# One core, a two-layer attention and feed-forward stack: the last layer's back pieces split in halves, one feed-forward unit per pair of heads, TensorE's back products one pair later, and two copies on ScalarE in the other order

## The reference, cut to what matters

```python
x = in_features                                   # (8, 512, 128) float32
x = x + attn_a(layernorm(x))                      # 1: attention over the full width, causal
x = x + ffn(layernorm(x))                         # 2
x = x + attn_b(layernorm(x), Wq, Wk, Wv, Wo, gamma, beta)   # 3: 16 heads of 64, causal
x = x + ffn(layernorm(x))                         # 4

def attn_b(x, ...):      # per head h: q, k, v = x Wq[h], x Wk[h], x Wv[h]
    attn = softmax(causal(q k^T / 8)); heads = concat(attn v)
    y = x + heads @ Wo
    return (y - mean(y)) * rsqrt(var(y) + 1e-3) * gamma + beta

def ffn(x):              # M = 64, INNER = 16
    s = x @ Win + bin_
    h = relu(s[..., None] * W1 + b1)
    return (einsum('btmh,mh->btm', h, W2) + b2) @ Wout + bout
```

## Time and profile before

| what | value |
|---|---|
| median of 3 runs | 915.17 us (912.46 to 921.88) |
| the profiled execution: its time / its span | 914.78 us / 912.9 us |
| granted TensorE clock, mean over the span | 0.905 |
| PE busy | 741.9 us (81%) |
| PEld / DVE / ACT / POOL busy | 533.9 / 659.8 / 571.5 / 533.4 us |
| heads stage: first pair of batch 0 starts / last pair of batch 7 starts | 235.8 / 859.1 us |

### The profile page before, as it was taken

One profiled execution on the slowest core, in us unless ns is written; L12 is line 12 of the kernel. 1 busy time (PEld: TensorE's weight loads), 2 busy tenths in 40 slices (PEclk: granted clock), 3 DMA queues, 4 the chain that ended last, 5 costly groups with the idle time before them and its releaser, 6 DMA issues. The chain is left out here.

```text
span 912.9 us, 21228 instructions
## 1 busy us (share of the span) xinstructions
PE 741.9 (81%) x7592; PEld 533.9 (58%) x7592; DVE 659.8 (72%) x1358; ACT 571.5 (63%) x1575; POOL 533.4 (58%) x496
## 2 busy tenths in 40 slices
PE   4476667633899998999899899989998998998843
PEld 3354555522466765766676567666766765666532
DVE  1488888763666787689678858967896896789654
ACT  0357666651667765776677668667767766776623
POOL 2156666443356567567666756665676667577631
PEclk9598878755999999999999999989999999999965
DMA  9111111101299888798579768959987898798630
GB/s 202 43 43 40 47 47 46 36 26 44 49 150 154 144 144 142 123 137 145 108 133 154 128 112 146 151 104 137 152 137 122 150 141 117 134 152 146 114 72 23
DMA packets 367142, 100.29 MB, mean 110 GB/s; under 512 B 347968, under 2 KB 364864, under 8 KB 367040
## 3 DMA queue, kind: packets, MB, share of 16 engines
q1 hardware_dynamic: 363776, 96.86, 61.6%
q10 hardware_dynamic: 3264, 2.10, 0.9%
HBM read 8.73 MB, written 2.10 MB: 12 GB/s over the span
## 5 line engine op out<-in xcount | busy, mean ns | idle before, releaser
L1003 POOL TENSOR_TENSOR prob_hl<-prob,prob_hl 128x768 f16<-128x768 f32 (+1 forms) x192 | 363.5, 1893 | 231.7 <-DVE prob_hl L947 231.6
L922 ACT ACTIVATE prob<-wide,neg_max 128x128 f32<-128x128 f32 (+3 forms) x512 | 264.8, 527 | 164.3 <-DVE neg_max L959 164.2
L959 DVE TENSOR_REDUCE neg_max<-wide 128x2 f32<-128x256 f32 (+3 forms) x256 | 204.7, 821 | 150.5 <-PE wide L836 149.0
L831 PE MATMUL wide<-k_sb,q_sb 64*128 64x128 f32 (+3 forms) x1024 | 195.2, 480 | 1.6 <-ACT k_sb L813 1.5
L856 PE MATMUL bank<-v_hi,prob_t 128*128 128x64 f16 x1280 | 136.4, 195 | 11.8 <-DMA prob_t<-prob_hl 10.9
L947 DVE CAST prob_hl<-prob 128x768 f16<-128x768 f32 (+1 forms) x192 | 135.9, 708 | 1.8 <-DMA prob_t<-prob_hl 1.0
L857 PE MATMUL bank<-v_lo,prob_t 128*128 128x64 f16 x1280 | 136.2, 195 | 0.0
L858 PE MATMUL bank<-v_hi,prob_t 128*128 128x64 f16 x1280 | 136.1, 195 | 0.0
L856 PEld LDWEIGHTS bank<-v_hi,prob_t 128*128 128x128 f16 x1280 | 118.4, 100 | 15.6 <-issue 11.7
L857 PEld LDWEIGHTS bank<-v_lo,prob_t 128*128 128x128 f16 x1280 | 116.5, 100 | 0.0
L858 PEld LDWEIGHTS bank<-v_hi,prob_t 128*128 128x128 f16 x1280 | 116.5, 100 | 0.0
(11 more groups left out here) (190 smaller groups left out, 1449.4 us busy)
## 6 DMA issues: line engine op xcount, KB each, us to landing
prob_t<-prob_hl SPq DMA_TRANSPOSE x384, 3.1
x_next<-in_L_attn_a_in_features SPq DMA_DIRECT2D x8, 256.0 KB, 3.1
x_attn<-in_L_attn_a_in_features SPq DMA_DIRECT2D x8, 256.0 KB, 3.1
x_sb<-x_done SPq DMA_DIRECT2D x8, 256.0 KB, 2.3
y_res<-bn_y SPq DMA_DIRECT2D x8, 256.0 KB, 2.3
out_x<-x_done SPq DMA_DIRECT2D x8, 256.0 KB, 2.6
wq_a<-in_L_attn_a_w_q ACTq DMA_DIRECT2D x1, 512.0 KB, 5.2
wq_b<-in_L_attn_b_Wq SPq DMA_DIRECT2D x1, 512.0 KB, 8.2
```

The lines of the kernel that those rows point to most:

```text
L831: pe.matmul(dst[:, h, c:c + m], q[e, i * P:(i + 1) * P], k[e, 0:m], start=(i == UNIT_ROWS[u][0]), stop=False)
L922: last = act.activation(prob_2[s][:, at:at + m], score_banks(p, s)[:, h, c:c + m], ACT.Exp, bias=neg_max[p % 2][:, h, i:i + 1], accum_out= ...
L959: last = dve.tensor_reduce(neg_max[p % 2][:, :, i:i + 1], score_banks(p, s)[:, :, c:c + m], AX.X, ALU.max, negate=True)
L1003: pool.tensor_tensor(prob_hl[u][:, w:2 * w], prob_2[u][:, 0:w], prob_hl[u][:, 0:w], ALU.subtract)\
```

## The change

The back's centre and residual on VectorE are cut in two halves of two blocks each, in steps 1 and 2 of p3 and in steps 0 and 1 of p4; the moments leave the statistics and go to step 0 of the next pair. On GpSimd ffn_xb goes behind unit 2 of p4, the second root to p5 unit 0, and the normalised tokens are made in halves behind units 1 and 2 of p5. TensorE's turn goes from p5 to p6, the product with Win from p6 to p7, the product with Wout (with x_done) from p7 to p0 of the next batch; all are still in step 2. The relus and adds of batch b - 2 are one per pair, in step 0: the relu of unit p in pair p, its add in the next pair, at the end of step 0's list on VectorE (the place is before the pieces of the back). Behind the last heads (b = 8) batch 6's units are taken one per step, and its output leaves in p3. On ScalarE the contexts are copied before the keys. DRAIN is one longer. The store follows one pair behind x_done.

```diff
@@ -722,12 +722,23 @@
...
         LAG = 4
-        DRAIN = 2 * HP + 1
-        RELU_PAIRS = (0, 1, 5, 6)
+        DRAIN = 2 * HP + 2
...
+        def unit_of_ffn(b, p, s):
...
+            if b == B:
+                return p * NU + s if p < NU else None
+            return p if s == 0 and 0 <= b - 2 < B else None
...
+        def leaves(b, p):
...
+            if b == B and p == 3:
+                return B - 2
+            return b - 3 if p == 0 and 0 <= b - 3 < B and b - 3 != B - 2 else None
...
@@ -790,11 +801,11 @@
...
             wait(pe, *(("k_sb", n) if done == "q_ps" else ("q_sb", n + 1)))
-            if done == "q_ps" and p == 7:
-                wait(pe, "g_xt", b)
             if done == "q_ps" and p == 0:
+                wait(pe, "g_xt", b - 1)
+            if done == "q_ps" and p == 1:
                 wait(pe, "g_s", b - 1)
-            if done == "q_ps" and p == 1:
+            if done == "q_ps" and p == 2:
...
             split_product(pe, QK, parts[:, p, 0, :], parts[:, p, 1, :], xt_hi[:, at], xt_lo[:, at])\
@@ -894,21 +905,21 @@
...
                         context_turn_tensor(pe, *earlier(b, p, 2))
-                if s == 2 and p == 5 and 0 <= b - 1 < B:
+                if s == 2 and p == 6 and 0 <= b - 1 < B:
                     back_turn_tensor(pe, b - 1)
-                if s == 2 and p == 6 and 0 <= b - 1 < B:
+                if s == 2 and p == 7 and 0 <= b - 1 < B:
                     back_s_tensor(pe, b - 1)
-                if s == 2 and p == 7 and 0 <= b - 2 < B:
-                    back_out_tensor(pe, b - 2)
+                if s == 2 and leaves(b, p) is not None:
+                    back_out_tensor(pe, leaves(b, p))
...
         def heads_scalar(act, b, p):
...
             for s in range(NU):
-                if s == 2 and p == 5 and 0 <= b - 1 < B:
+                if s == 2 and p == 6 and 0 <= b - 1 < B:
                     back_xt_scalar(act, b - 1)
-                if s == 2 and p == 6 and 0 <= b - 1 < B:
+                if s == 2 and p == 7 and 0 <= b - 1 < B:
...
                     wait(act, f"m{s}", n + 1)
@@ -926,16 +937,17 @@
...
                     queries_scalar(act, *later(b, p))
-                if s == 1 and pair_exists(*later(b, p)):
-                    keys_scalar(act, *later(b, p))
...
                     act.copy(ctx_t[:, :], MB[:, :]).then_inc(sem("ctx_t"), 1)
+                if s == 1 and pair_exists(*later(b, p)):
+                    keys_scalar(act, *later(b, p))
...
                     values_scalar(act, b + 1, p, MB)
-                if p in RELU_PAIRS and s < 2 and 0 <= b - 2 < B:
-                    back_relu_scalar(act, b - 2, 2 * RELU_PAIRS.index(p) + s)
+                j = unit_of_ffn(b, p, s)
+                if j is not None and j < J:
+                    back_relu_scalar(act, b - 2, j)
...
@@ -977,22 +989,25 @@
...
                         values_vector(dve, bv + 1, pv, MB)
+                back_adds_vector(dve, b, p, s)
...
                     back_statistics(dve, y_norm, lambda i: y_res[:, (b - 1) * QB + i, :], "gy", b - 1)
-                if s == 1 and p == 3 and 0 <= b - 1 < B:
-                    back_center_vector(dve, b - 1)
-                if s == 0 and p == 4 and 0 <= b - 1 < B:
-                    back_residual_vector(dve, b - 1)
+                if s == 0 and p == 3 and 0 <= b - 1 < B:
+                    back_moments(dve, y_norm, "gy", b - 1)
+                if s > 0 and p == 3 and 0 <= b - 1 < B:
+                    back_center_vector(dve, b - 1, s - 1)
+                if s < 2 and p == 4 and 0 <= b - 1 < B:
+                    back_residual_vector(dve, b - 1, s)
                 if s == 2 and p == 4 and 0 <= b - 1 < B:
-                    wait(dve, "g_x", b)
+                    wait(dve, "g_x", 2 * b)
                     back_statistics(dve, ffn_norm, lambda i: x_ffn[:, i, :], "gf", b - 1)
-                if p in RELU_PAIRS and s > 0 and 0 <= b - 2 < B:
-                    back_add_vector(dve, b - 2, 2 * RELU_PAIRS.index(p) + s - 1)
-                if s == 2 and p == 7 and 0 <= b - 2 < B:
-                    back_done_vector(dve, b - 2)
+                if s == 0 and p == 5 and 0 <= b - 1 < B:
+                    back_moments(dve, ffn_norm, "gf", b - 1)
+                if s == 2 and leaves(b, p) is not None:
+                    back_done_vector(dve, leaves(b, p))
...
             n = number(b, p)
@@ -1020,9 +1035,10 @@
...
                         .then_inc(sem(f"pt{u}"), 16)
-            if p == 0 and 0 <= b - 3 < B:
-                wait(sp, "g_done", b - 2)
-                sp.dma_start(out_tiles[:, seq(b - 3), :], x_done[:, :, :]).then_inc(sem("stored"), 16)
+            if p > 0 and leaves(b, p - 1) is not None:
+                c = leaves(b, p - 1)
+                wait(sp, "g_done", c + 1)
+                sp.dma_start(out_tiles[:, seq(c), :], x_done[:, :, :]).then_inc(sem("stored"), 16)
         def back_sum_vector(dve, c):
@@ -1036,6 +1052,8 @@
...
+        def back_moments(dve, norm, done, c):
...
                 last = dve.bn_aggr(norm.mean_var[:, i, :], norm.stats[:, i, :])
@@ -1049,24 +1067,35 @@
...
-        def back_center_vector(dve, c):
+        def back_center_vector(dve, c, half):
             wait(dve, "gy_mv", c + 1)
-            for i in range(QB):
+            for i in range(half * QB // 2, (half + 1) * QB // 2):
...
-        def back_residual_vector(dve, c):
-            wait(dve, "g_c", c + 1)
+        def back_residual_vector(dve, c, half):
+            wait(dve, "g_c", 2 * c + 2)
...
             wait(dve, "g_xb", c)
-            for i in range(QB):
+            for i in range(half * QB // 2, (half + 1) * QB // 2):
...
+        def back_adds_vector(dve, b, p, s):
...
+            if s == 0 and p == 0 and 0 <= b - 3 < B and b - 3 != B - 2:
+                back_add_vector(dve, b - 3, J - 1)
+            if b == B:
+                j = unit_of_ffn(b, p, s)
+                if j is not None and 0 < j <= J:
+                    back_add_vector(dve, b - 2, j - 1)
+            elif s == 0 and p > 0 and 0 <= b - 2 < B:
+                back_add_vector(dve, b - 2, p - 1)
...
             wait(dve, "g_relu", J * c + j + 1)
@@ -1094,27 +1123,28 @@
...
                 wait(pool, "kept", 16 * B)
-                wait(pool, "g_x", c)
+                wait(pool, "g_x", 2 * c)
...
                 back_rstd_gpsimd(pool, y_norm, "gy", c)
-            if p == 4 and u == 1:
-                wait(pool, "g_x", c + 1)
+            if p == 4 and u == 2:
+                wait(pool, "g_x", 2 * c + 2)
...
                     .then_inc(sem("g_xb"), 1)
-            if p == 4 and u == 2:
+            if p == 5 and u == 0:
...
                     .then_inc(sem("gf_nm"), 1)
-            if p == 5 and u == 0:
-                wait(pool, "gf_rstd", c + 1)
-                wait(pool, "gf_nm", c + 1)
-                wait(pool, "g_xt_ps", c)
-                for i in range(QB):
+            if p == 5 and u > 0:
+                if u == 1:
+                    wait(pool, "gf_rstd", c + 1)
+                    wait(pool, "gf_nm", c + 1)
+                    wait(pool, "g_xt_ps", c)
+                for i in range((u - 1) * QB // 2, u * QB // 2):
...
                 last.then_inc(sem("g_y"), 1)
@@ -1123,21 +1153,21 @@
...
         def back_turn_tensor(pe, c):
-            wait(pe, "g_y", c + 1)
-            wait(pe, "g_done", c - 1)
-            wait(pe, "k_sb", bank_left(c + 1, 5))
+            wait(pe, "g_y", 2 * c + 2)
+            wait(pe, "g_done", c if c == B - 1 else c - 1)
+            wait(pe, "k_sb", bank_left(c + 1, 6))
...
         def back_s_tensor(pe, c):
             wait(pe, "g_xt", c + 1)
-            wait(pe, "k_sb", bank_left(c + 1, 6))
+            wait(pe, "k_sb", bank_left(c + 1, 7))
...
         def back_out_tensor(pe, c):
             wait(pe, "g_add", J * c + J)
-            wait(pe, "g_s", min(c + 2, B))
-            wait(pe, "k_sb", bank_left(c + 2, 7))
+            wait(pe, "g_s", min(c + 2, B) if c != B - 2 else c + 1)
+            wait(pe, "k_sb", bank_left(c + 3, 0))
...
                                  start=True, stop=True)

```

## The result

The changed kernel takes 921.37 us, median of 20 runs (918.82 to 923.41), beside 916.60 us for the kernel before (20 runs, 911.0 to 924.44). The ratio is 1.0049, 95% interval 1.0029 to 1.0068: slower by half a per cent, which is clear of the scatter of these runs but inside the one per cent that the prediction counts as no change. Predicted were 919. The profiled execution took 921.27 us (span 919.5, clock 0.916).

The account below looks back on a forecast made before the run. Bound: TensorE, with waits for the context copy (10.2 us) and GpSimd's tokens (19.8). Sum from 914.8: 5.8 - 1.3 - 2.0 - 0.3 + 0.2 + 2 = +4.4, taken as 919 us; range 888 to 934.

Parts of the forecast that it names:

- The add is held: In step 0 behind v_lo, the add waits for GpSimd's split, ending at +5.68; row maxima start 0.87 us late.
- rival A: The add is not held; undisturbed pairs stay 8.93 us, a full batch 76.6 to 76.8, time 886; chance 0.22.
- Pairs: Predicted lengths of p0 to p7, a full batch 82.6 us; batches 3 to 6 together +5.8.
- p1: Pair without back work: with the held add and swapped copies it grows by 0.3 to 9.23 us.
- p6: Pair with half the tokens ahead of its unit 2, keys at +9.45: 10.8 us, before 11.34.
- The swap: On ScalarE, contexts copied before keys: bounds of -0.46 us where the context is late, 0 elsewhere.
- Halves pay a hold each: Centre and residual on VectorE: one held operation per half, before one per piece; p4 11.5 us, before 10.84.
- The clock: TensorE's clock drops, 1.55 us each; the new batches are charged +2 us in all, bounds 0 and 19.
- rival B: TensorE's clock: two stretches a batch fall to 1.2 GHz, 18.6 us instead of 2, time 936; one, 926; chance 0.29.
- The end: Last batch's units no longer queue, 1.7 us saved, against +1.9 for adds and output: +0.2, bounds -1.5 and +2.
- Rival C: Transfers of probabilities set the pace; worth 0 to -3 us, time 916; chance 0.45 together with the forecast.
- D: Only the removal of waits bites: a batch 73.6 us, 47 saved, time 868; chance 0.04.

Follow-up runs that it names:

- e1: The changed kernel with each add moved from step 0 to step 1 of the same pair, directly behind the cast: 895.98 us, ratio 0.9767.
- e2: The changed kernel with the add still in step 0, but ahead of the reciprocal and contexts, directly behind the cast of unit 2: 897.56 us, ratio 0.9789.
- e3: The changed kernel with the keys copied before the contexts again, alone: 913.05 us, ratio 0.9968.
- e8: The kernel before with one part of the change alone, the contexts copied ahead of the keys: 920.84 us, ratio 1.004.
- e4: The changed kernel with centre whole in step 1 of p3 and residual whole in step 0 of p4: 915.75 us, ratio 0.9991.
- e10: The changed kernel with the halves of centre and residual ahead of the cast of their step, adds staying in step 0: 907.70 us, ratio 0.9905.
- e9: e5 with GpSimd's x + beta one split earlier, behind unit 0 of p2 instead of unit 1: 871.62 us, ratio 0.95.
- e11: The changed kernel with GpSimd's split of unit 2 replaced by a one-input copy (output not the reference's): 892.65 us, ratio 0.9734.
- e5: The changed kernel with adds in step 1 and the halves of centre and residual ahead of the cast of their step: 876.37 us, ratio 0.9554.

## Why the prediction was right, point by point

- **The add is held** (forecast against rival A). Right, in every time: end +5.68, maxima +5.60, contexts +8.33 predicted and +8.29 measured, keys +8.78 both, p2 9.23 and 9.24. e1 and e2 show the cause. Rival A's time, 886, is 10 to 12 below what they reach when it is made true, 896 and 898. But the prediction's "whenever it comes second" is too wide, and the trace before already shows it (batch 2, p5; POOL, then DVE):

```profile
440.77 2.54 POOL L1118 TENSOR_SCALAR fn_y<-x_ffn,fn_neg_mean,fn_rstd 128x128 f32<-128x128 f32 x4
...
441.98 0.74 DVE L1079 SCALAR_TENSOR_TENSOR ffn_g<-relu_two,w,ffn_g 128x512 f32<-128x512 f32 x1
```

  This add starts inside GpSimd's tokens and takes its plain time, and the four operations of GpSimd take 2.54 instead of 4 x 0.45. The sum was not hurt, since no term of it rests on an add beside the tokens.
- **Pairs**, predicted / measured on the mean: p0 10.6 / 10.68, p1 9.23 / 8.97, p2 9.25 / 9.23, p3 10.35 / 10.32, p4 11.5 / 11.58, p5 10.3 / 10.18, p6 10.8 / 11.30, p7 10.55 / 10.87; 82.6 / 83.13. Batch 1 75.2 / 75.55, batch 2 80.9 / 81.16, batch 7 68.4 / 68.38.
- **p1 was mis-sized.** Its add is unit 0, a tensor_scalar of one tensor; held to 0.29 behind the split, as the earlier trace rows already had it, not 0.55, and 1.31 long.
- **p6 was mis-sized by 0.5.** I took half the tokens as 0.9, twice the 0.447 of one. They took 1.31, since the first of the two, 0.88 long, runs beside a held cast of VectorE. That pushed the split on by 0.4 and held the add for 2.21 (POOL, DVE, ACT, PE; the pair starts at 609.78):

```profile
612.61 1.31 POOL L1148 TENSOR_SCALAR fn_y<-x_ffn,fn_neg_mean,fn_rstd 128x128 f32<-128x128 f32 x2
613.89 2.14 POOL L1018 TENSOR_TENSOR prob_hl<-prob,prob_hl 128x1024 f16<-128x1024 f32 x1
...
614.36 2.21 DVE L1108 SCALAR_TENSOR_TENSOR ffn_g<-relu_two,w,ffn_g 128x512 f32<-128x512 f32 x1
...
619.08 0.60 ACT L824 COPY k_sb<-bank 128x512 f32<-128x512 f32 x1
...
619.82 0.63 PE L194 MATMUL bank<-ident,fn_y 128*128 128x128 f32 x4 [1.82 <-ACT k_sb L824]
```

  Keys at +9.90, not +9.45, the turn at +10.04. p7's miss (10.87 for 10.55) is mostly the one pair of batch 5 named below.
- **The swap**: its bounds, "-0.46 where the context is late, 0 elsewhere", leave out that it can cost time. The keys' delay was in the sum for p0, p6, p7, but not set against the swap: e3 is 8 us faster without it, and e8 slower with it alone.
- **Halves pay a hold each.** Right (p4), but e4 shows that making them whole saves 0.7 of p5 and hardly anything of p4, while their place ahead of the cast saves 1.75 of p4 (e10).
- **The clock** (+2; rival B). Not needed in the profiled execution: batches 1 and 2 show 1.00, 3 to 6 0.99. The longest wait is not the 1.1 to 1.3 that I had, but the 1.82 at the turn in p6; even so only one pair of batches 3 to 6 lost by it (p7 of batch 5, 11.57 for 10.65 in batch 4). With waits of 3.8 in p5 of e8, that pair shows 0.86 to 0.98 in batches 3 to 6, the lower of the two levels, 1.2 GHz, for a part of it. The length of a wait alone doesn't decide it: in p4 of e1 the clock falls behind waits of 1.4 in batches 2, 3 and 6, and in p4 of e2 waits as long leave it at 1.00. When it falls the prediction did not work out, and the runs leave it open.
- **The end** came out 1.2 shorter (52.62 after the last pair's start, 53.80 before), not 0.2 longer, inside its bounds; which of its terms was off no run separates. The heads stage starts 2.8 later (238.71, before 235.87), though nothing ahead of it was edited: in the twelve other traces its start lies between 235.8 and 238.8 too, so this is chance.
- **The sum** for the profiled execution: start 2.84, batches 0, 1 and 2 -0.04, -1.66 and -1.00, batches 3 to 6 8.00, batch 7 -0.37, end -1.18: +6.6 of span (919.5 - 912.9), 6.5 of time (921.27 - 914.78), where +4.4 was predicted. Of the difference 2.2 is the four full batches; the stage's start (+2.8), the clock (-2) and the end (-1.4) nearly cancel, and that is luck. By the medians the change is +4.8.
- **Rival C**: the wait for transfers fell from 10.9 to 4.7 us; what the time has of it no run separates. **D**, 868, is what e9 comes near to (871.6) once hardly an add, centre or residual is held; casts still are, in e9 too.

## What to carry to other kernels

Before placing an operation of VectorE that reads two tensors of SBUF, or its cast, look at what GpSimd is doing at that moment of the pair, not at whether VectorE has room: the same add was worth 24 us by starting 1.3 us earlier in the pair (e2). A piece cut in halves is held once per half; put each half ahead of the cast that starts GpSimd. And before shortening something ahead of a wait, ask when the other side of the wait is ready: if it does not move, the gain is paid out as a longer wait, and the clock may be lost with it.

## What the runs showed of the hardware that was not expected

Not every operation of GpSimd that reads SBUF holds VectorE. The subtraction with two inputs, the one-input copy of e11, x + beta and x + output bias do (the last held an add of e11 to 1.70). The root on 128x4 does not: in e9 four centre operations start 0.25 to 0.53 us inside one and take their plain 0.34. In e5 (p6 of batch 4; POOL, then DVE) an add starts inside GpSimd's normalised tokens, a tensor_scalar:

```profile
593.04 1.69 POOL L1148 TENSOR_SCALAR fn_y<-x_ffn,fn_neg_mean,fn_rstd 128x128 f32<-128x128 f32 x2
...
593.39 0.75 DVE L1108 SCALAR_TENSOR_TENSOR ffn_g<-relu_two,w,ffn_g 128x512 f32<-128x512 f32 x1
```

The add takes its plain 0.75, while the two operations of GpSimd take 1.69 instead of 2 x 0.447, their median; so it is in six batches (the add 0.75, the first of the two 1.25 to 1.27). VectorE came second, and GpSimd lost. It loses time in other rows too: the split behind e2's earlier add, where VectorE came first, takes 2.58 instead of 2.13. The Trainium skill (SBUF — State Buffer, section "SBUF: two separate sides") calls the ports that the two engines share an exclusive lock, for the whole instruction of whoever starts first, against any GpSimd operation that reads SBUF: the copy of e11 agrees (the add ends 0.55 behind it), the row above does not. Why this operation gives way was not tried. VectorE's maxima and its lower values, which read PSUM, were never held beside a split: in the changed kernel the maxima of 128x768 take 0.92 to 0.97 us with a split going or without, and the lower values 0.67 to 0.68 in all 49 cases beside one.

Nor did I expect how exactly one number holds: 0.55 us from the end of GpSimd's operation to the end of the held add, in 41 of the changed kernel's adds (0.545 to 0.552). It is another number for other operations: 0.15 for one of centre, 0.28 to 0.29 for the first unit's tensor_scalar.
